# Sum over the states of a selective scan by transposes that accumulate, in a two-layer kernel on one core

## The reference, cut to what matters

```
for each token t:                       # the scan, 128 channels d, 64 states n
    dA = exp(d_t[..., None] * A)
    h  = dA * h + (d_t * u_t)[..., None] * b_t[:, None, :]
    y  = einsum('bdn,bn->bd', h, c_t)   # the sum over the 64 states
left  = ys + u * D                      # the skip
gated = left * silu(right)
s     = x + gated @ W_down + b_down
# experts: scores = softmax(hidden @ gate_w.T), for each of 16 experts the 512 best tokens of a sequence,
# g = gelu(x_tok @ Wg.T) * (x_tok @ Wu.T), out += (g @ Wd.T) * weight, plus one shared expert over all tokens
x = x + s * silu(moe)
```

## Time and profile before

| | us |
|---|---|
| median of 3 runs | 4906.13 |
| lowest and highest of them | 4898.42, 4906.37 |
| the profiled execution, its own time | 4907.92 |
| its span, first to last instruction | 4906.2 |

### The profile page before, as it was taken

The page is one execution under the profiler, slowest core; times in us unless marked ns, Lnnn a source line. Parts: engine busy times, 40 slices in busy tenths (PEclk is TensorE's granted clock), DMA queues, the critical chain, the costliest instruction groups (busy, mean ns, idle before and its releaser), DMA issues. The chain is left out here.

```text
span 4906.2 us, 63777 instructions
## 1 busy us (share of the span) xinstructions
PE 4415.1 (90%) x22548; PEld 3244.1 (66%) x22548; DVE 3473.6 (71%) x4975; ACT 2581.4 (53%) x4855; POOL 2585.0 (53%) x1858
## 2 busy tenths in 40 slices
PE   8899999978999999889999967789989998999985
PEld 6788888867888888666666534556656565656652
DVE  5466666654666666537887769888887888788888
ACT  6544444446444444366666653266556665666665
POOL 3122222233122210136666637778888888888988
PEclk9999999988999999889999968899999999999998
DMA  2022222221122210223443321345555555556558
GB/s 88 26 85 87 70 85 87 85 73 50 52 87 82 75 42 22 68 74 129 137 138 119 126 86 62 93 161 170 180 167 168 165 185 170 159 166 177 181 177 313
DMA packets 271473, 572.62 MB, mean 117 GB/s; under 512 B 37169, under 2 KB 157746, under 8 KB 271154
## 3 DMA queue, kind: packets, MB, share of 16 engines
q1 hardware_dynamic: 246578, 534.98, 32.4%
q0 software_dynamic: 24576, 33.57, 3.9%
HBM read 445.64 MB, written 122.81 MB: 116 GB/s over the span
## 5 line engine op out<-in xcount | busy, mean ns | idle before, releaser
L1535 POOL TENSOR_TENSOR scan_drive_sb<-scan_b_wide_sb,scan_du_sb 128x1024 f32<-128x1024 f32 x512 | 1292.6, 2553 | 373.4 <-DVE scan_h_sb L1446 362.8
L1446 DVE TENSOR_TENSOR_SCAN scan_h_sb<-decay_bank,scan_state_sb,scan_drive_sb 128x512 f32<-128x512 f32 x896 | 1116.5, 1268 | 104.5 <-ACT decay_bank L1770 101.8
L1631 PE MATMUL y_bank<-scan_ch_sb,identity_sb 128*128 128x512 f32 x2048 | 1075.7, 620 | 3.6 <-DVE scan_ch_sb L1453 3.2
L1770 ACT ACTIVATE decay_bank<-scan_delta_sb,a_neg_sb 128x512 f32<-128x512 f32 x1024 | 699.9, 686 | 369.1 <-DVE scan_h_sb L1446 366.4
L1453 DVE TENSOR_TENSOR scan_ch_sb<-c_pair,scan_h_sb 128x1024 f32<-128x1024 f32 x512 | 615.2, 1202 | 116.5 <-PE c_pair L1622 115.4
L958 PE MATMUL ybank<-v_low_hi_lo_sb,pt_hi_b_sb 128*128 128x384 f32 x2048 | 663.5, 358 | 21.9 <-DVE pt_lo_b_sb L838 15.0
L838 DVE TENSOR_TENSOR pt_lo_b_sb<-pt,pt_hi_b_sb 128x512 fp32r<-128x512 f32 x512 | 352.9, 690 | 413.8 <-ACT pt_hi_b_sb L1001 413.8
L992 ACT ACTIVATE p_b_sb<-scores,softmax_cols_b_sb 128x1024 f32<-128x1024 f32 x256 | 286.0, 1117 | 550.8 <-DVE softmax_cols_b_sb L832 411.3
L959 PE MATMUL ybank<-v_low_hi_lo_sb,pt_lo_b_sb 128*128 128x256 f32 x2048 | 572.3, 279 | 0.0
L1001 ACT ACTIVATE pt_hi_b_sb<-pt 128x512 fp32r<-128x512 f32 x512 | 306.2, 598 | 413.4 <-PE pt L946 413.4
L1622 PE MATMUL c_pair<-scan_cc_sb,select_state_sb 128*128 128x512 f32 x1024 | 379.1, 452 | 145.1 <-DVE scan_ch_sb L1453 143.6
(11 more groups left out here) (322 smaller groups left out, 9895.2 us busy)
## 6 DMA issues: line engine op xcount, KB each, us to landing
scan_b_wide_sb<-b_scratch SPq DMA_DIRECT2D x512, 512.0 KB, 3.9
w_hi_scratch<-split_hi_sb SPq DMA_DIRECT2D x51, 512.0 KB, 2.8
w_lo_scratch<-split_lo_sb SPq DMA_DIRECT2D x51, 512.0 KB, 4.1
expert_hi_sb<-w_hi_scratch SPq DMA_DIRECT2D x48, 512.0 KB, 5.3
expert_lo_sb<-w_lo_scratch SPq DMA_DIRECT2D x48, 512.0 KB, 6.2
x_b_sb<-x SPq DMA_DIRECT2D x16, 512.0 KB, 3.9
g_scratch<-g_out_b_sb SPq DMA_DIRECT2D x16, 512.0 KB, 3.2
split_raw_sb<-WgT SPq DMA_DIRECT2D x16, 512.0 KB, 5.3
```

What stands on the lines that cost most here:

```text
L1446: e.tensor_tensor_scan(k.h[i % H_BUFFERS][:, j, :], k.decay_banks[S % DECAY_BANKS][:, :], k.drive[i % DRIVE_BUFFERS][:, j, :], start, ALU. ...
L1535: e.tensor_tensor(k.drive[i % DRIVE_BUFFERS][:, :, :], k.b_wide[i % B_BUFFERS][:, :, :], k.du[c % 2][:, :].unsqueeze(1).broadcast_to([P, P ...
L1631: e.matmul(k.y_bank[:, :], consts.identity[:, :], k.ch[i % CH_BUFFERS][:, j, :], start=(n == 0), stop=(n == STATES - 1)).then_inc(k.s_y, 1)
L1770: e.activation(k.decay_banks[S % DECAY_BANKS][:, :], k.delta[c % 2][:, :], ACT.Exp, scale=wt.a[:, n:n + 1]).then_inc(k.s_decay, 1)
```

## The change

The sum over the states is formed turned round: each 128 tokens of a state's `ch` become the stationary operand of a transpose (four for a state, with the identity as the moving operand), and all 64 states' transposes add in `y_bank`. ScalarE copies the bank out once per chunk (`y_out`), TensorE turns it back with four transposes into a bank of `Fills` (`y_turned`), and `skip` reads that bank. The steps of `down` go from 10 to 12. In the choice of tokens the rate is 1.0 up to step 35 (the bits, the ties and the ranks) and 1.3 behind it, and each bit's count product stands one step later in TensorE's stream.

```diff
--- before.py
+++ after.py
@@ -1191,8 +1191,10 @@
 
 
 
-PAIRS_AT = (5, 7)
-DOWN_STEPS = 10
+Y_TURNED_AT = 1
+GATED_AT = 3
+PAIRS_AT = (7, 9)
+DOWN_STEPS = 12
 
 
 def part(table, step):
@@ -1265,7 +1267,7 @@
         self.s_ch = self.sem("ch")
         self.s_kept = self.sem("state_kept")
         self.s_y = self.sem("y_sum")
-        self.s_skip = self.sem("skip")
+        self.s_y_out = self.sem("y_out")
         self.s_gated = self.sem("y_gated")
         self.s_g_hi = self.sem("g_hi")
         self.s_g_lo = self.sem("g_lo")
@@ -1453,10 +1455,8 @@
         e.tensor_tensor(k.ch[i % CH_BUFFERS][:, :, :], k.c_bank[:, :, :], k.h[i % H_BUFFERS][:, :, :], ALU.mult).then_inc(k.s_ch, 1)
 
     def skip(c):
-        w.wait_ge(k.s_y, STATES * (c + 1))
-        w.wait_ge(k.s_delta, min(c + 2, ALL_CHUNKS))
-        w.wait_ge(k.s_g_lo, c)
-        e.scalar_tensor_tensor(k.temp[3][:, :], k.u[c % 2][:, :], wt.skip[:, 0:1], k.y_bank[:, :], ALU.mult, ALU.add).then_inc(k.s_skip, 1)
+        fills.wait_filled(w, "y", c)
+        e.scalar_tensor_tensor(k.temp[3][:, :], k.u[c % 2][:, :], wt.skip[:, 0:1], fills.bank("y", c), ALU.mult, ALU.add).then_inc(fills.emptied("y", c), 1)
 
     def residual(c, pair):
         fills.wait_filled(w, "down", c, pair)
@@ -1466,8 +1466,9 @@
                         ALU.add).then_inc(fills.emptied("down", c, pair), 1)
 
     def down(c):
-        skip(c)
         for s in range(DOWN_STEPS):
+            if s == Y_TURNED_AT + 1:
+                skip(c)
             pair = part(PAIRS_AT, s - 1)
             if pair is not None:
                 residual(c, pair)
@@ -1536,7 +1537,7 @@
                         k.du[c % 2][:, :].unsqueeze(1).broadcast_to([P, PAIR, CHUNK]), ALU.mult).then_inc(k.s_drive, 1)
 
     def gated(c):
-        w.wait_ge(k.s_skip, c + 1)
+        fills.wait_emptied(w, "y", c)
         w.wait_ge(k.s_gate, c + 1)
         e.tensor_tensor(X, X, k.gate[c % 2][:, :], ALU.mult).then_inc(k.s_gated, 1)
 
@@ -1546,9 +1547,9 @@
 
     def down(c):
         for s in range(DOWN_STEPS):
-            if s == 1:
+            if s == GATED_AT:
                 gated(c)
-            if s == 3:
+            if s == GATED_AT + 2:
                 gated_lower(c)
             yield
 
@@ -1627,8 +1628,20 @@
         c, n = divmod(S, STATES)
         w.wait_ge(k.s_ch, i + 1)
         if n == 0:
-            w.wait_ge(k.s_skip, c)
-        e.matmul(k.y_bank[:, :], consts.identity[:, :], k.ch[i % CH_BUFFERS][:, j, :], start=(n == 0), stop=(n == STATES - 1)).then_inc(k.s_y, 1)
+            w.wait_ge(k.s_y_out, c)
+        for t in range(GT):
+            tokens = slice(t * P, (t + 1) * P)
+            last = e.matmul(k.y_bank[:, tokens], k.ch[i % CH_BUFFERS][:, j, tokens], consts.identity[:, :], start=(n == 0 and t == 0),
+                            stop=(n == STATES - 1), is_transpose=True, skip_group_check=True)
+        last.then_inc(k.s_y, 1)
+
+    def y_turned(c):
+        w.wait_ge(k.s_y_out, c + 1)
+        bank = fills.take(w, "y", c)
+        for t in range(GT):
+            tokens = slice(t * P, (t + 1) * P)
+            last = e.transpose(bank[:, tokens], k.temp[3][:, tokens], consts.identity[:, :])
+        last.then_inc(fills.filled("y", c), 1)
 
     def down_pair(c, pair):
         w.wait_ge(k.s_g_lo, c + 1)
@@ -1645,6 +1658,8 @@
 
     def down(c):
         for s in range(DOWN_STEPS):
+            if s == Y_TURNED_AT:
+                y_turned(c)
             pair = part(PAIRS_AT, s)
             if pair is not None:
                 down_pair(c, pair)
@@ -1692,7 +1707,8 @@
         fills.wait_emptied(w, "gate", c)
         e.activation(k.gate[c % 2][:, :], k.gate[c % 2][:, :], ACT.Silu).then_inc(k.s_gate, 1)
         fills.wait_filled(w, "conv", c)
-        w.wait_ge(k.s_skip, c - 1)
+        if c > 1:
+            fills.wait_emptied(w, "y", c - 2)
         w.wait_ge(k.s_du, c - 1)
         e.activation(k.u[c % 2][:, :], fills.bank("conv", c), ACT.Silu, bias=wt.conv_b[:, 0:1]).then_inc(fills.emptied("conv", c), 1)
 
@@ -1781,9 +1797,17 @@
             fills.wait_filled(w, "down", c - 1, 1)
         e.activation(k.u_hi[:, :], X, ACT.Copy).then_inc(k.s_g_hi, 1)
 
+    def y_out(c):
+        w.wait_ge(k.s_y, STATES * (c + 1))
+        w.wait_ge(k.s_delta, min(c + 2, ALL_CHUNKS))
+        w.wait_ge(k.s_g_lo, c)
+        e.activation(X, k.y_bank[:, :], ACT.Copy).then_inc(k.s_y_out, 1)
+
     def down(c):
         for s in range(DOWN_STEPS):
-            if s == 2:
+            if s == 0:
+                y_out(c)
+            if s == GATED_AT + 1:
                 gated_upper(c)
             yield
 
@@ -1797,7 +1821,8 @@
 HB = HIDDEN // P
 ROWS16, COLS32 = 16, 32
 SCORE_BITS = 30
-CHOOSE_RATE = 1.3
+BITS_RATE = 1.0
+LISTS_RATE = 1.3
 SHARED_RATE = 1.0
 MOE_RATE = 1.0
 ALL_GROUPS = TOKENS // GROUP
@@ -1937,8 +1962,11 @@
 def moe_order(pace, prepare, shared, choose, experts, last):
     yield from prepare
     yield from pipeline(range(ALL_GROUPS), shared)
-    pace.rate = CHOOSE_RATE
-    yield from choose
+    pace.rate = BITS_RATE
+    for step, _ in enumerate(choose):
+        if step == BACK_STEP:
+            pace.rate = LISTS_RATE
+        yield
     pace.rate = MOE_RATE
     yield from pipeline(range(ALL_GROUPS, BLOCKS), experts)
     yield from last
@@ -2499,11 +2527,13 @@
                 turned = e.transpose(bank[:, j * P:(j + 1) * P], turns(k.scores, half)[:, :, j], consts.identity[:, :])
             turned.then_inc(fills.filled("by_list", half), 1)
         yield
+        yield
         w.wait_ge(k.s_made, 2)
         for r in range(SCORE_BITS):
             w.wait_ge(k.s_signs, r + 1)
             from_counts(k.group, k.count[:, :], "bit", r)
-            yield
+            if r < SCORE_BITS - 1:
+                yield
         w.wait_ge(k.s_pick, PICK_TIES + 2)
         from_counts(k.group, k.count[:, :], "ties")
         yield
```

## The result

The changed kernel takes 4832.45 us (median of 4 runs, 4824.35 to 4833.94), the kernel before 4902.95 us. The ratio is 0.9855 [0.9843, 0.9867]: **70.5 us faster, where 196 were forecast**, and 27 us above the upper end of the range. The profiled execution took 4831.77 us.

A forecast was written before the change was run, and what follows sets the result against it. TensorE was taken to bound the shared expert's and experts' stages, with a second engine close. Savings of 91 + 90 + 7 + 10 - 2 = 196 us gave 4710 us, range 4630 to 4805.

The forecast's parts named there:

- the rival of transposes as full products: Sum over states: each transpose costs two records with weight loads, 1.6 us a state, kernel slower at 5536 us; chance 0.03.
- The step that failed: Shared expert and experts: item time is the busiest engine's time over 0.93, giving 4.51 and 4.68 us.
- (B): Experiments' theory: items are set one by one, by VectorE's work or by waits that TensorE's speed does not touch.
- Shared expert: Shared expert's stage: 120 items fall from 5.27 to 4.51 us, 91 us less; bounds 61 to 114.
- Experts: Experts' stage: GpSimd becomes the bound, 284 items fall from 5.00 to 4.68 us, 90 us less; bounds 0 to 145.
- Bits: Bit search: 3.1 us a bit, 93 against 100 us, 7 less; bounds 25 less to 17 more.
- The rate: Choice: 4 items move from combination into search, 16.5 us less there, 6 more for its later start; net 10 less.
- What is added once a chunk: ScalarE's copy, four transposes, a bank, two handovers: taken as 0, only 2 us after the last chunk.
- (C): Experiments' theory: what is added once a chunk, or the turn of two banks in `Fills`, takes the gain back.
- GpSimd as the bound already: Experts' stage: GpSimd already bounds it, so the experts give 0 and the whole is 4800 us; chance 0.17.
- The falling clock: Large stages: less-worked TensorE is granted a clock of 0.85, 137 us less in all, 4769 us; chance 0.13.
- (D): Experiments' theory: TensorE's lower clock takes the gain back.

The follow-up runs named there:

- the next cut: Changed kernel with one transpose instead of four for every state but a chunk's first, so part of the sum is left out: 4811.17 us.
- A third bank: Three banks instead of two in `Fills`, the first state's c lost: kernel before 4835.44 us, changed kernel 4750.25 us.
- the run without the Gelus' tables: Changed kernel with Exp in place of Gelu in the routed blocks, so no table is changed for them: 4770.52 us.
- the run of the sum alone: Changed kernel with the search's part (rates, count product a step later) undone, only the sum by transposes left: 4820.55 us.
- the search alone: Kernel before with only the choice's rates and the count product a step later: 4901.99 us, ratio 1.0002.
- the last experiments: Sum by transposes alone with `delta` three and `du` two steps later, 4790.15 us; that plus two decay banks and three in `Fills`, 4803.52 us.

## Why the prediction was wrong in size

**The prices were right.** A state's four transposes take 0.35 us by their starts (forecast 0.36) and some 0.44 with what they add to the next product (forecast 0.44), the bound for a weight load more did not come, and the rival of transposes as full products is out. TensorE's item fell to 514.15/118 = 4.36 and 1161.77/288 = 4.03 us, against 4.07 and 3.80 forecast; the clock, 0.92 for 0.96 and 0.94 for 0.98, makes 0.18 and 0.16 us of the differences (4.36 x 0.04/0.96, 4.03 x 0.04/0.98). The remaining 0.11 and 0.07 us were not traced.

**The step that failed** is "An engine that bounds a stage here is busy 93% of it", with 4.19/0.93 and 4.36/0.93 behind it. It makes one engine the bound of all items of a stage. The runs show no such engine, before or after. What came back for each us of busy time taken away: TensorE 71/304 = 0.23 for the change and 21/217 = 0.10 for the next cut; GpSimd 17/131 = 0.13; VectorE 44/247 = 0.18 before the change and 75/247 = 0.30 after it; ScalarE, the least busy of the four in that stage, 62/92 = 0.67. (With 10 us of uncertainty the 0.10 and 0.13 are good to 0.05 and 0.08.) A third bank, with no work taken from any engine, gave 69 us before the change: TensorE at 93% did not bound that kernel. With the timeline this reads as (B): 56% of the items in the experts' stage held no wait of VectorE before the change, and the rest held one of about 2 us. TensorE's relief could shorten only those of the rest whose wait was for TensorE, and the wait for `c_pair` fell by 26 us in this stage, which gained 30. How much of a wait a given saving ends is not derived here. I had read the waits for decays as standing behind TensorE's banks in ScalarE's queue. In the changed kernel, where they are 71.6 us, the run without the Gelus' tables has 17.4 left: most of them stand behind ScalarE's own batch of Gelus and tables. For the 64.9 us of the kernel before this was not run.

The Trainium skill (Perfetto Trace Analysis, Identifying the Most-Contended Engine) says that matmul busy time is not a good measure of how close a kernel is to its limit. These runs agree with that much: 93% busy returned 0.23 us for each us saved. The page's reason, that pipelined instructions look smaller in the trace, is not what failed here.

**Term by term.** Shared expert: 35 us for 91, below the term's own lower bound of 61 (41 in the run of the sum alone). Experts: 30 for 90, within its bounds of 0 to 145 (50 in the run of the sum alone). Bits: 3 us more instead of 7 less (3.5 us from sign to sign, forecast 3.1), within its bounds. I had said that TensorE would no longer wait for the signs and that the wait would be VectorE's: TensorE still waited 45.7 us for them (78.6 before), and VectorE's wait for the count at the decision fell, from 25.3 us in 19 to 19.5 in 18. The rate: worth nothing, since the search alone came to +0.2 us. The end: 16 us less, from the shorter stretch behind the experts. What is added once a chunk: I took nothing. It was not tried alone, but its waits in the changed kernel's trace are small: ScalarE's copy waits 7.1 us in all for the last sum, the next sum 4.9 for the copy, and the skip 2.5 for the turned bank, 15 us together, where VectorE's skip waited 8.9 us before. The third bank shows that the turn was no new cost (69 us before, 82 after), so (C) falls for the missing 125 us.

**The rivals.** GpSimd as the bound already would have given 4800 us, and its place is refuted: in the changed kernel cutting its work by 131 us brought 17, and in the kernel before relief of VectorE (44 us) and a third bank (69 us) paid with GpSimd's work untouched. The falling clock had the right sign and the wrong size: 0.04 in the large stages where it took 0.11 and 0.13, and it was at 0.88 in a kernel that was faster. It accounts for part of the busy time only, so (D) falls as the main cause; its own share of the missing time was not measured. By the rule of the Trainium skill that I set beside it (TensorE: Matmul & The Clock Gate, Part 4: PE-mode transpose) the transposes should not have run at the full clock. No run holds a stage of transposes alone. Those at 2402.86 us stand 0.11 us apart, (0.60 - 0.27)/3, at a granted clock of 1.0, where the earlier trace rows has 0.21 at the low clock. In the mixed stages the granted clock stayed at 0.92 and 0.94, and fell when three of four transposes were taken out. Of what I named as signs of being wrong, none came outright: four transposes take 0.44 us, a bit 3.5, and GpSimd, which was to rise above 89%, stands at 89.2%. What the new profile was to show failed more clearly: GpSimd over 92%, VectorE over 90% in the shared stage (83%), c's wait halved (69.8 to 43.5), 4.5 and 4.7 us an item. The range missed because all its cases but "nothing" and the full products shared the failed step.

**Still open:** what stands behind the 43.5 us for which VectorE still waits for the spread c, its second longest wait after decays; how much of a wait a saving on one engine ends, which is what a forecast would need; why the gains of the last experiments don't add.

## What to carry to other kernels

Before you divide a stage's busy time by its share, take the next engine's timeline apart at one recurring instruction and count the intervals in which it never stands: relief of the busiest engine leaves those alone. It does not follow that relief of the next engine shortens them in full; here it gave 44 and 75 us for 247. The remaining intervals are worth what their waits are worth, and a wait that comes once a batch can be ended by moving one instruction a few steps: at `delta` that gave 30 us. Relief can be tested before the change is built: leave out part of one engine's work and see what comes back.

## What the runs showed of the hardware

- Transposes of fp32 that add in their bank follow each other every 0.11 us for 128x128 at the full clock, one record each, 0.44 us for four, against 0.85 us for the product of 128x512 with the identity that gives the same sum.
- A table load takes 1.283 us every time, and the Gelus begin as it ends (3709.55 + 1.28 against 3710.84). The Trainium skill (ScalarE: Activation LUTs, What ACT_TABLE_LOAD costs) gives the same 1283 ns and adds about 1380 ns of drain for a switch; no such gap stands in this timeline.
- VectorE's `delta`, the same instruction 16 times, took between 0.69 and 2.88 us (median 1.76); what lengthens it was not looked into.
- In the bits (2806 to 2907 us) TensorE's granted clock was 0.50, which is the low level of 1.2 GHz throughout, with TensorE busy 69% of the stretch; before it was 0.64 at 66%. In the combination it was 0.70 (4700 to 4780 us, busy 61%) against 0.93 before (4741 to 4869 us, busy 70%).
